# Sixteen sequences through four conditioned layers on one core: the expert's label read once per sequence, and new order lists for the loop and the close

## The reference

```
L0  y = x @ weight[subject].T + bias[subject]
L1  zX * laplace_x(x) + zY * laplace_y(x) + zR * x * (1 - x)
L2  16 heads of 16: queries from the side input, keys and values from x (masked by length) and one
    own key and value per query from the side input; softmax; @ Wo + bo
L3  three feed-forward experts 256 -> 1024 -> 256 with relu: two shared, one picked by the sequence's
    label; each token's sum weighted by softmax(relu(first rows @ g1) @ g2)
```

## Time and profile before

| | |
|---|---|
| median of 3 runs | 972.61 us |
| the profiled execution | 973.26 us, its span 971.4 us |
| opening, up to the first turn's H0 | 77.4 us |
| 14 turns, H0 to H0 | 799.8 us, 57.1 each; the last 13 take 738.1 |
| close | 94.3 us |
| busy PE, PE's weight loads, DVE, ACT, POOL | 95, 92, 76, 77, 64% |

### The profile page before, as it was taken

One profiled execution on the slowest core, in us unless ns is written; L12 is line 12 of the kernel. 1 busy time (PEld: TensorE's weight loads), 2 busy tenths in 40 slices (PEclk: granted clock), 3 DMA queues, 4 the chain that ended last, 5 costly groups with the idle time before them and its releaser, 6 DMA issues.

```text
span 971.4 us, 28400 instructions
## 1 busy us (share of the span) xinstructions
PE 923.5 (95%) x9138; PEld 891.7 (92%) x9138; DVE 734.1 (76%) x1518; ACT 751.3 (77%) x1682; POOL 625.1 (64%) x576
## 2 busy tenths in 40 slices
...
GB/s 189 199 175 189 141 174 152 157 157 132 180 154 176 138 159 160 135 173 155 179 141 157 157 140 173 149 174 152 157 157 140 173 151 176 149 157 124 148 94 11
DMA packets 361503, 149.47 MB, mean 154 GB/s; under 512 B 282340, under 2 KB 360452, under 8 KB 361476
## 3 DMA queue, kind: packets, MB, share of 16 engines
...
q10 hardware_dynamic: 432, 0.39, 0.1%
...
...
## 4 chain that ended last, share of the span: by engine, by line
PE 62%; SPq 11%; DVE 7%; DMA 7%; ACT 6%; issue 5%; POOL 2%; ACTq 0%; DVEq 0%
PE out L760 7%; PE out L761 7%; PE out L762 7%; PE hid L760 6%; PE hid L762 6%; PE hid L761 6%; SPq L629 5%; PE front L760 4%; PE front L762 4%; PE front L761 4%; PE front L870 3%; DMA ksT<-parts_own 3%; DMA turned_own<-parts_own 3%; ACT prob_own L1131 3%; PE pv L827 2%
## 5 line engine op out<-in xcount | busy, mean ns | idle before, releaser
L1649 POOL TENSOR_TENSOR parts_own<-prob_own,parts_own 128x512 f16<-128x512 f32 x133 | 158.0, 1188 | 133.2 <-ACT parts_own L1137 133.0
L760 PE MATMUL hid<-x_hi,exp_hi 128*128 128x256 f32 x768 | 232.8, 303 | 5.5 <-DVE x_lo L1422 5.4
L1315 DVE TENSOR_REDUCE neg_max<-front 128x2 f32<-128x512 f32 x244 | 164.8, 687 | 85.3 <-PE front L870 82.8
L760 PE MATMUL out<-hid_hi,exp_hi 128*128 128x256 f32 x768 | 226.1, 294 | 2.3 <-ACT e_out L1160 2.3
L762 PE MATMUL hid<-x_hi,exp_lo 128*128 128x256 f32 x768 | 221.8, 289 | 0.0
L761 PE MATMUL hid<-x_lo,exp_hi 128*128 128x256 f32 x768 | 221.7, 289 | 0.0
L761 PE MATMUL out<-hid_lo,exp_hi 128*128 128x256 f32 x768 | 214.1, 279 | 0.0
L762 PE MATMUL out<-hid_hi,exp_lo 128*128 128x256 f32 x768 | 214.0, 279 | 0.0
L1131 ACT ACTIVATE prob_own<-front,neg_max 128x256 f32<-128x256 f32 x476 | 198.0, 482 | 13.0 <-DVE neg_max L1315 9.9
L1579 POOL TENSOR_TENSOR exp_lo<-raw,exp_hi 128x512 fp32r<-128x512 f32 x128 | 170.7, 1345 | 26.5 <-ACT exp_hi L1153 26.5
L1426 DVE SCALAR_TENSOR_TENSOR hid_lo<-hid,hid_hi 128x512 fp32r<-128x512 f32 x192 | 130.6, 686 | 48.0 <-ACT hid_hi L1175 45.8
...
## 6 DMA issues: line engine op xcount, KB each, us to landing
...
```

The costliest lines, as they stand in the source:

```text
L760: nc.tensor.matmul(acc, w_hi, a_hi, start=first, stop=False)
L1315: nc.vector.tensor_reduce(neg_max[:, :, h:h + 1], psum, AX_X, ALU.max, negate=True).then_inc(max_done, 1)
L1649: nc.gpsimd.tensor_tensor(of_head[:, 2 * S:4 * S], slot_of(prob, more_prob, i, h), of_head[:, 0:2 * S], ALU.subtract).then_inc(prob_split_ ...
```

## The change

The label is read in a step of its own, `label`, ahead of `T0` in the loop's list and in the close's (where `label.15` reads the last sequence's); the four `wo` steps use the register. `wi_load` still reads it. The five lists of the loop and the five of the close are new. The opening's lists, the arithmetic and the buffers are unchanged. The loop's lists, and the two of the close that the prediction speaks of:

```
 PE_BODY
-H0 H1 S0 S1 P0 S2 H2 S3 P1 H3 S4 H4 S5 P2 V0 S6 H5 V1 V2 S7 P3 x1 H6 V3 S8 V4 S9 P4 P5 q V5 S10 H7 V6 V7 S11 P6 S12 H8 S13 H9 V8 V9 S14
-P7 V10 S15 H10 H11 lap V11 V12 P8 P9 kp ks V13 V14 V15 vs P10 aT P11 vp wo gate self logits
+H0 H1 S0 S1 P0 H2 S2 S3 H3 P1 S4 H4 V0 S5 P2 V1 S6 H5 V2 S7 P3 V3 x1 H6 V4 S8 S9 P4 P5 q V5 V6 S10 H7 S11 P6 V7 S12 H8 H9 V8 V9 S13 P7
+S14 V10 S15 H10 H11 lap V11 V12 P8 P9 kp ks V13 V14 V15 vs P10 aT P11 wo gate vp logits self
 ACT_BODY
-H0 wi0 wi1 H1 E0 C0 E1 wi2 H2 C1 E2 wi3 C2 E3 H3 E4 C3 C4 x_parts w_parts E5 E6 H4 C5 s_parts H5 E7 C6 C7 P3 x1_parts x3_keep react E8
-E9 own0 H6 C8 wo0 C9 q wo1 E10 H7 C10 wo2 E11 E12 C11 C12 wo3 H8 E13 H9 C13 E14 P7 C14 E15 C15 x2_parts qa H10 H11 own1 kp kq ks vs qb
-aT P11 x3_parts x2b logits vp sum
+H0 wi0 wi1 H1 E0 C0 E1 wi2 H2 C1 E2 wi3 C2 E3 H3 C3 E4 C4 x_parts w_parts E5 E6 C5 H4 C6 P3 H5 s_parts E7 wo0 x1_parts react C7 E8 H6
+wo1 C8 E9 C9 own0 q E10 H7 C10 wo2 E11 E12 C11 C12 H8 wo3 E13 H9 E14 C13 C14 P7 E15 C15 own1 qa x2_parts x3_keep H10 H11 kp kq vs qb aT
+P11 ks x3_parts x2b vp logits sum
 DVE_BODY
-H0 S0 S1 S2 H1 H2 E1 S3 S4 H3 x_parts E3 S5 S6 S7 E5 H4 H5 x1 E7 S8 gate0a S9 own0 x1_parts react S10 H6 E9 S11 S12 H7 half E11 S13 H8
-S14 H9 S15 E13 own1 lap x2_parts gate0b H10 H11 kp att k3 gate1 aT gate2 wo relu x3_parts logits self mix scale vp
+H0 S0 H1 S1 S2 S3 E1 H2 x_parts S4 H3 E3 S5 S6 S7 E5 H4 gate0a x1 H5 S8 S9 own0 E7 react H6 S10 E9 S11 H7 S12 half x1_parts E11 S13 H8
+S14 H9 S15 E13 own1 lap x2_parts H10 H11 kp att gate0b gate1 aT gate2 wo relu k3 x3_parts logits mix self scale vp
 POOL_BODY
-E0 wi0 wi1 E2 wi2 E4 x_parts w_parts s_parts wi3 E6 x1 E8 wo0 E10 wo1 E12 wo2 wo3 E14 E15 qa own norm qb ks sum vp
+E0 wi0 wi1 E2 wi2 E4 x_parts w_parts wi3 E6 s_parts x1 E8 wo0 wo1 E10 E12 wo2 wo3 E14 E15 own qa norm qb ks sum vp
 SP_BODY
-T0 T1 wo0 T2 wo1 T3 T4 T5 wo2 T6 T7 wo3 T8 T9 T10 T11 T12 T13 T14 T15 wi_load kp k3 load sum
+label T0 T1 T2 T3 T4 wo0 wo1 T5 wo2 T6 T7 wo3 T8 T9 T10 T11 T12 T13 T14 T15 wi_load kp k3 load sum
 CLOSE_PE (its first half)
-H0 H1 S0 S1 P0 S2 S3 H2 S4 H3 S5 P1 S6 H4 V0 V1 S7 P2 P3 S8 V2 S9 H5 V3 V4 S10 P4 S11 H6 V5 S12 P5 S13 H7 S14 V6 V7 S15 P6 P7 V8 V9 H8
+H0 H1 S0 S1 P0 S2 H2 S3 S4 H3 P1 S5 H4 S6 V0 P2 S7 V1 V2 S8 P3 S9 H5 S10 P4 V3 V4 S11 H6 S12 H7 V5 V6 S13 P5 S14 V7 P6 P7 V8 S15 H8 V9
 CLOSE_SP
-T0 T1 T2 T3 T4 wo0 wo1 wo2 T5 T6 T7 T8 T9 wo3 T10 T11 T12 T13 T14 T15 wi_load wo0.15 wo1.15 sum wo2.15 wo3.15 sum.15
+label T0 T1 T2 wo0 wo1 label.15 T3 T4 wo2 T5 T6 T7 T8 T9 T10 T11 wo3 T12 T13 T14 T15 wi_load wo0.15 wo1.15 sum wo2.15 wo3.15 sum.15
 
+            chosen = {}
+
...
+                elif name == "label":
+                    chosen[i if isinstance(i, int) else None] = chooser(label_sb, i, wo.shape[0])
                 elif name[0:2] == "wo":
                     n = int(name[2])
-                    kind = chooser(label_sb, i, wo.shape[0])
                     wait(sp, w_split, PARTS, i, SHARED_POOL + n + 1)
-                    load_wo(kind, n)
+                    load_wo(chosen[i if isinstance(i, int) else None], n)
```

More of the change, by code:

```diff
@@ L145 @@
 CLOSE_PE = list(closing("""
-H0 H1 S0 S1 P0 S2 S3 H2 S4 H3 S5 P1 S6 H4 V0 V1 S7 P2 P3 S8 V2 S9 H5 V3 V4 S10 P4 S11 H6 V5 S12 P5 S13 H7 S14 V6 V7 S15 P6 P7 V8 V9 H8
-H9 V10 V11 P8 H10 H11 V12 V13 V14 V15 P9 P10 aT P11 wo fill6 H0.15 gate H1.15 P0.15 logits H2.15 H3.15 P1.15 P2.15 H4.15 P3.15 H5.15
-H6.15 P4.15 P5.15 H7.15 H8.15 P6.15 P7.15 H9.15 H10.15 P8.15 P9.15 H11.15 P10.15 P11.15 gate_a.15 fill3 gate_b.15 fill2 logits.15
+H0 H1 S0 S1 P0 S2 H2 S3 S4 H3 P1 S5 H4 S6 V0 P2 S7 V1 V2 S8 P3 S9 H5 S10 P4 V3 V4 S11 H6 S12 H7 V5 V6 S13 P5 S14 V7 P6 P7 V8 S15 H8 V9
+V10 V11 H9 P8 V12 H10 H11 V13 V14 V15 P9 P10 aT P11 wo fill6 H0.15 H1.15 gate P0.15 H2.15 logits H3.15 P1.15 H4.15 P2.15 P3.15 H5.15
+H6.15 P4.15 P5.15 H7.15 H8.15 P6.15 P7.15 H9.15 P8.15 H10.15 H11.15 P9.15 fill2 P10.15 P11.15 gate_a.15 gate_b.15 logits.15 fill3
 """))
 CLOSE_ACT = list(closing("""
-H0 wi0 wi1 H1 E0 E1 C0 C1 E2 E3 C2 H2 E4 C3 E5 C4 H3 C5 wi2 wi3 E6 E7 H4 C6 C7 P3 E8 E9 C8 C9 H5 E10 E11 C10 H6 C11 own0 E12 E13 H7 wo0
-C12 E14 C13 C14 E15 wo1 own1 H8 P7 C15 wo2 H9 H10 wo3 H11 aT x3_keep P11 x3_parts H0.15 H1.15 wi0.15 logits wi1.15 wi2.15 H2.15 wi3.15
+H0 wi0 wi1 H1 E0 C0 E1 E2 C1 C2 H2 wi2 E3 wi3 E4 C3 H3 E5 C4 E6 C5 H4 E7 C6 E8 P3 C7 E9 C8 H5 own0 E10 C9 H6 E11 C10 C11 E12 E13 H7 wo0
+E14 C12 C13 C14 P7 x3_keep H8 own1 E15 wo1 C15 H9 wo2 H10 wo3 H11 aT wi0.15 P11 x3_parts H0.15 wi1.15 wi2.15 wi3.15 H1.15 H2.15 logits
 sum H3.15 H4.15 P3.15 wo0.15 H5.15 wo1.15 wo2.15 H6.15 H7.15 H8.15 P7.15 H9.15 wo3.15 H10.15 H11.15 logits.15 first.15
```

8 lines of the change are left out of this document (4 added, 4 removed).

## The result

The changed kernel takes **938.35 us** (median of 4 runs, 937.25 to 939.30), the kernel before 972.09 in the same runs (970.94 to 976.15). The ratio is 0.9645, 95% interval 0.9615 to 0.9675: 34 us less. The profiled execution took 938.34 us, its span is 936.5 and its mean granted clock 0.997 (before: 973.26, 971.4, 0.979). The forecast was 949.

A forecast was written before the change was run, and what follows sets the result against it. PE sets the time, busy 923.5 of 971.4 us. Gains of 0.7 + 0.13 + 0.41 + 0.3 - 0.1 = 1.44 a turn, 20.2 over 14 turns, plus 3.5 in the close, make 23.7 less: 949 us, range 938 to 965.

The forecast's parts named there:

- the end of the turn: From `P11` to the next `S0`: `vp` fills the hole behind `wo`, `H0` no earlier, `S0` waits less; gain 0.13 a turn.
- the third transpose: SP's label read between `T1` and `T2` goes, so `T2` is issued 1.2 earlier; gain 0.7 a turn.
- the half clock: Start of the turn: `vp`'s dense matmuls in the thin stretch keep PE's clock up; gain 0.41 a turn.
- S2's bank, `e_out`: Rest of the turn: `S2` behind `H2` waits for no bank, ACT copies `e_out` before `H5`; gain 0.3 together.
- waits not seen: Waits that the new lists bring elsewhere in the turn, set against the gains at 0.1 a turn.
- the close, once: After the loop: `wo0` and `wo1` ahead of `T3`, one `wo2` before `T5`; 3.5 of 4.1 us won.
- The three saved ones further down stood where SP had time, so I cost them at nothing: SP's list: two label reads a turn replace five; the three saved further down gain nothing.
- The thin stretches still halve the clock: Rival, PE around the turn's end: all 14 turns lose 0.82 to half clock; 960 us, chance 0.12.
- the transposes are bound elsewhere: Rival: `T2` may wait for POOL's splits, not SP, and `V0` to `V2` wait too; 967 us, chance 0.13.
- DVE and POOL block each other: Rival, turn's end: POOL's own-scores product meets `k3` and `x_lo`; 13 us back, 962, chance 0.10.
- Slower: Rival: the chain from `logits` to `T0` slips 3.0 a turn, and every later transpose with it; 984 us, chance 0.06.
- One sign of being wrong: On PE: a wait for a transpose of `V0` or `V1` shows up; the other such sign was turns over 56.

The follow-up runs named there:

- the one with a wait of 1.8 ahead of `wo`: The changed kernel with DVE's `k3` moved back ahead of `gate0b` and `gate1`: 973.1 us.
- the kernel with 1.3 of idle ahead of `gate`: The changed kernel with ACT's `aT` ahead of `qb` and DVE's `gate0b` ahead of `H10`: 955.0 us.
- the old front half: The kernel before with SP's new lists and the new end of the turn on PE, ACT and DVE, the rest of their lists as before: 938.5 us.
- the first experiment: The kernel before with the label read once, ahead of `T0` (`label.15` ahead of `wo0.15` in the close), all other lists as before: 951.0 us.

## Why the prediction was right and wrong

The direction was right, and most of what was forecast happened; the sizes were too small. 949 was said and 938.35 came, at the fast end of the range. Two terms of the sum failed: the end of the turn, put at 0.13 a turn, measured 0.46, and the third transpose, put at 0.7, measured 0.87. Step by step, per turn:

| step of the prediction | forecast | measured |
|---|---|---|
| the third transpose | 0.7 | 0.87 (mean of 13 turns, with SP's lists alone) |
| the end of the turn | 0.13 | 0.46 (turns at full clock from 55.05 to 54.59) |
| the half clock | 0.41 | 0.43 (0.80 in seven of 13, none left) |
| S2's bank, `e_out` | 0.3 | 0 and 0.32, the latter by the label's reads |
| waits not seen | -0.1 | none found in the 13 turns |
| sum | 1.44 | 2.08; the turns themselves give 2.14 |
| the close, once | 3.5 | 3.5 |

The forecast for the profiled execution was 949.6 and it took 938.3. Of these 11.3 us, 9.1 lie in the 13 turns, 1.3 in the first turn (2.7 less where 1.44 was said) and 0.9 in the opening, which is luck.

- **The third transpose: the size failed, at the 0.15 that was left over.** The price was right: the forecast took 0.72 + 0.16 = 0.88 for what the late `T2` cost, and 0.87 was won. The step that failed is "`T2` issued 11.8 after `H0` lands at 15.4. So I leave 0.15". It was issued at 11.97 with the old PE list, when PE asked for it at 15.71, and at 11.45 with the new, when PE asked at 15.0, and it landed 3.08 later and not 3.6, at 15.06 and 14.5. The 3.65 was read in the kernel before, where a piece's load is issued just ahead of `T2`; in the new order none is. (The list of steps in that sentence has four hidden steps behind `H1`, not five; its 15.3 comes out with four.)
- **The end of the turn: the size failed.** The new wait ahead of `wo` was said to be 0.6: `P11` lengthened by 0.58. `H0` was said to come no earlier: 6.72 for 6.65. The step that failed is the one behind it, "until 6.25 after `wo`, 3.1 after `H0`. Gain there: 0.15". DVE's last `vp` ended at 411.45, 5.89 after `wo`'s end (405.56) and 2.74 after `H0`. `S0` starts 0.34 behind that step in both kernels, so every bit by which it comes nearer to `H0` is won: 3.27 - 2.74 = 0.53 and not 0.15. Of the 0.36 that the walk was too long, 0.19 is there at the end of `x_lo` (2.56 after `wo`, 2.75 said). The prediction gave this term a point and no bounds.
- **The half clock: right.** The two kernels with only SP's lists changed kept four and five such turns of 13, so 0.31 of the 0.43 came with the new end. Nine kernels here have `vp` between `gate` and `logits`: eight had none in 13 turns, and the one with a wait of 1.8 ahead of `wo` had five. The five kernels that end `gate self logits` had between 4 and 13. The Trainium skill (TensorE: Matmul & The Clock Gate, HAM oscillation) ties the halving to idle gaps. The traces bear it out in part: with the old end, 1.5 of idle ahead of `vp` went with 13 halved turns where there were four without it, and with the new end only the kernel where `wo` waited 1.8 lost the clock. But idle time alone does not decide: the kernel with 1.3 of idle ahead of `gate` kept its clock, the one with 0.4 of idle in a stretch of small matmuls lost it.
- **S2 and `e_out`: the sum right by luck, the cause wrong.** `S2` behind `H2` shortened `P0` from 1.69 to 1.50, and yet the turn was as long as with the old front half, 54.64 and 54.63: that 0.2 was not won. The wait for `e_out` was put at 0.1, the idle time in the list of waits (1.6 us in 13 turns); from start to start it was 0.32, and it went with the label's reads and not with ACT's new order.
- **"The three saved ones further down stood where SP had time, so I cost them at nothing":** wrong in both orders. In the old one the read of `wo1` held `T3` and `T4` by 0.7 and with them ACT, a part of the 0.32 above by the trace. In the new one the four reads of the `wo` steps in place of one cost 20 us.
- **The close: right in its size**, 94.3 to 90.75. The wait of 3.08 is gone, and the longest for a transpose is 1.6.
- **The rivals.** *The thin stretches still halve the clock* fell with the profile after, *the transposes are bound elsewhere* with the first experiment. *DVE and POOL block each other* did not happen, by the 0.28 that the walk had found (0.3 was said). Its price was set too low: 13 us was said; taking the meeting away from the three terms was worth 16, half of it by the clock, and bringing two of them about cost 17 net of what the edit won. The rule of the Trainium skill (SBUF — State Buffer, Summary: rules for kernel authors), that the second of such a pair fully waits for the first, holds in the four kernels shown here (the one before and three experiments): a gate term that meets POOL's product ends 0.27 to 0.29 after it each time. *Slower* had no ground: in the last 13 turns PE waits for no transpose.
- **Signs.** Those named came: the third transpose without wait, the new wait on `ak_lo` of 0.4, none on `x_lo`, no half clock at a turn's start. Two came out past their mark, as above: no wait listed ahead of `S0` where 0.3 to 0.5 was said, and turns of 54.6 where 55.3 was. One sign of being wrong came too, once: in the first turn PE waits 1.2 for the transpose of `V0`, which it now asks for sooner, and that turn is 2.8 longer than with the old front half.
